# Idle TensorE products of the identity in three stretches of a two-layer gated attention and expert kernel

## What is computed

```python
x = x + tanh(g_xattn[0]) * attention0(layernorm(x), ctx)       # 16 heads attend to each other within a token
x = x + tanh(g_ffn[0])   * ffn0(layernorm(x))                  # 1024 wide, activations rounded to fp8
x = x + tanh(g_xattn[1]) * attention1(ctx, layernorm(x), mask) # 16 heads of 16, softmax over 512 keys
x = x + tanh(g_ffn[1])   * moe(layernorm(x))                   # 8 experts, top 2, 256 -> 1024 -> 256

# attention1: q, k, v = layernorm(. @ W + b) * scale + bias ; softmax(where(mask, q k / 4, -1e9)) v @ Wo + bo
# moe: logits = x @ gate_w + gate_b ; top 2 of the softmax, renormalised
#      out = sum over the two of weight * (silu(x @ w1) * (x @ w3)) @ w2
```

## Time and profile before

| what | value |
|---|---|
| median of 3 runs | 2118.34 us (2112.92 to 2119.60) |
| profiled execution | 2116.76 us |
| its span | 2115.0 us |
| mean granted TensorE clock | 0.954 of full |
| PE busy | 1902.5 us, 90% |
| DVE busy | 1563.4 us, 74% |
| ACT / POOL busy | 1156.6 us, 55% / 921.6 us, 44% |

### The profile page before, as it was taken

How to read it: one execution, slowest core, us unless ns; L and a number is a source line. 1 busy time by engine, 2 the same in 40 slices (tenths; PEclk the granted TensorE clock), 3 DMA queues, 4 the chain that set the end, 5 groups by cost and what they waited for, 6 DMA issues and landing times. The chain is left out here.

```text
span 2115.0 us, 36023 instructions
## 1 busy us (share of the span) xinstructions
PE 1902.5 (90%) x11968; PEld 1329.2 (63%) x11968; DVE 1563.4 (74%) x3233; ACT 1156.6 (55%) x2414; POOL 921.6 (44%) x683
## 2 busy tenths in 40 slices
PE   5899999986669999998999999929999999999998
PEld 2566666665223434343434343419999999999998
DVE  7999999993466677776767778547777777777775
ACT  2356665655335555655555655515555666666663
POOL 6999999981633334352434331112222222222222
PEclk8899999998679999999999999959999999999999
DMA  5222222210425151524242441037666666666661
GB/s 172 111 91 111 88 111 111 84 58 1 112 57 123 31 125 60 112 66 105 78 100 91 89 118 34 31 104 254 223 223 217 217 226 228 226 230 226 220 213 60
DMA packets 140067, 271.47 MB, mean 128 GB/s; under 512 B 13915, under 2 KB 91823, under 8 KB 134066
## 3 DMA queue, kind: packets, MB, share of 16 engines
q1 hardware_dynamic: 128812, 244.55, 37.6%
q0 software_dynamic: 10624, 25.26, 3.2%
q10 hardware_dynamic: 518, 0.27, 0.0%
HBM read 201.96 MB, written 71.39 MB: 129 GB/s over the span
## 5 line engine op out<-in xcount | busy, mean ns | idle before, releaser
L1447 DVE CUSTOM_DVE_ANT_0 x_dump<-x_ps,x_bias_q 128x512 bf16<-128x512 f32 x512 | 353.0, 689 | 103.5 <-PE x_ps L1140 90.4
L1316 ACT ACTIVATE x_PT<-x_ps 128x512 f32<-128x512 f32 x512 | 292.2, 601 | 231.5 <-PE x_ps L1155 228.7
L1929 ACT ACTIVATE X<-m_ps 128x256 f32<-128x256 f32 x312 | 119.1, 382 | 226.0 <-PE m_ps L1866 226.0
L1833 POOL DMA_INDIRECT out_dram<-e_y,e_label x78 | 78.9, 1011 | 362.5 <-DVE e_y L1985 350.6
L1140 PE MATMUL x_ps<-x_KS,x_QS 96*128 96x512 bf16 x512 | 200.7, 393 | 26.2 <-DVE x_mx L1447 25.7
L1154 PE MATMUL x_ps<-x_bias_k,x_ident_b 128*128 128x512 bf16 x512 | 196.8, 384 | 2.2 <-issue 1.1
L1155 PE MATMUL x_ps<-x_QS,x_KS 98*128 98x512 bf16 x512 | 196.5, 384 | 0.0
L1968 DVE TENSOR_TENSOR X<-X,m_ps 128x256 f32<-128x256 f32 x312 | 120.5, 416 | 97.0 <-ACT X L1929 92.5
L1866 PE MATMUL m_ps<-e_x_lo,m_hi 128*128 128x256 f32 x640 | 181.3, 283 | 1.5 <-DVE e_x_lo L1953 1.5
L1866 PE MATMUL m_ps<-e_x_hi,m_hi 128*128 128x256 f32 x640 | 180.9, 283 | 0.0
L1866 PE MATMUL m_ps<-e_x_hi,m_lo 128*128 128x256 f32 x640 | 180.7, 282 | 0.0
(11 more groups left out here) (309 smaller groups left out, 5462.9 us busy)
## 6 DMA issues: line engine op xcount, KB each, us to landing
m_raw<-in_L_ffn_w_dram SPq DMA_DIRECT2D x117, 1024.0 KB, 5.2
expert_in<-a_blank SPq DMA_DIRECT2D x34, 1032.0 KB, 4.3
parts<-x_part SPq DMA_DIRECT2D x24, 512.0 KB, 3.8
m_x<-expert_in SPq DMA_DIRECT2D x39, 258.0 KB, 4.8
next_mask_k<-in_maskT_dram SPq DMA_DIRECT2D x32, 256.0 KB, 2.6
next_mask_q<-in_mask_dram SPq DMA_DIRECT2D x29, 256.0 KB, 2.8
x_KS<-parts SPq DMA_DIRECT2D x16, 384.0 KB, 11.0
x_QS<-parts SPq DMA_DIRECT2D x8, 576.0 KB, 6.4
```

Of the source, the lines that this page charges most:

```text
L1316: act.activation(PT[unit % 2][:, k, :], ps_st[e % 3], ACT.Exp, scale=DH ** -0.5).then_inc(exp_done, 1)
L1447: dve.tensor_tensor_reduce(out=dump[:, :], in0=ps_max[m % 2], in1=bias_q[b % 2][:, q, :], scale=1.0, scalar=NEG, op0=ALU.add, op1=ALU.max, ...
L1929: act.activation(silu[f % 2], ps_h[f % 4][:, 0:BLK], ACT.Silu).then_inc(silu_done, 1)
```

## The change

A helper `stay_busy` on PE issues float32 products of the identity with itself, 128x128, into a bank that is not in use. The products wait for nothing of their own, they only stand in PE's order:

- In the units before 0: 6 ahead of `turn_x` of tiles 0 to 3 (unit -14), 38 ahead of tile 4's (-10), 9 ahead of tile 4's `turn_qk` (-8), 8 ahead of tile 5's `turn_x` (-6), 6 ahead of tile 5's `turn_qk` (-4), 6 ahead of tile 6's `turn_x` (-2), 4 each ahead of `project_kv(4)` and `project_kv(5)`, and one behind each of the maxima 0 to 23: 105 products. They write `ps_o`, and so PE also waits for the first of DVE's constants.
- In the last batch: 2 ahead of each of the four outputs, 10 and 2 ahead of the two turns, 3 ahead of each of the two logits, 10 ahead of the ranks: 36 products.
- In the block ahead of the experts: 16 products once ACT has made the high part of the second weight matrix.

```diff
--- before.py
+++ after.py
@@ -692,6 +692,7 @@
 Q_RUNS = ((0, 3, 0), (3, 2, 0), (5, 1, 0))
 K_RUNS = ((0, 2, 0), (2, 2, 0), (4, 1, 0), (5, 1, 2))
 READS = len(Q_RUNS) + len(K_RUNS)
+BUSY_BEFORE = {-14: 6, -10: 38, -8: 9, -6: 8, -4: 6, -2: 6}
 FIRST_UNIT, LAST_UNIT = -16, NUNITS + 15
 
 
@@ -888,6 +889,10 @@
                     if e[0] in ("spread", "output", "logits", "ranks"):
                         m_freed[e] = len(m_freed) + 2
 
+        final = TPB * (BATCH - 1)
+        BUSY_AT_LAST = {**{("output", final + j): 2 for j in range(TPB)}, ("turn", final // 2): 10, ("logits", final // 2): 3,
+                        ("turn", final // 2 + 1): 2, ("logits", final // 2 + 1): 3, ("ranks", BATCH - 1): 10}
+
         def wait(eng, semaphore, count):
 
             if count > 0:
@@ -1098,6 +1103,11 @@
 
         @block.tensor
         def _(pe):
+            def stay_busy(products, out):
+
+                for _ in range(products):
+                    pe.matmul(out, ident_f[:, :], ident_f[:, :], start=True, stop=True)
+
             def project_kv(n):
                 wait(pe, c_in[n % 2], 16 * (n // 2))
                 if n >= EARLY:
@@ -1170,6 +1180,8 @@
 
             def bank_m(event):
                 what, n = event
+                if event in BUSY_AT_LAST:
+                    stay_busy(BUSY_AT_LAST[event], ps_max[0][:, 0:P])
                 if what == "rows":
                     pe.wait_ge(max_split, n + 1)
                 elif what == "sums":
@@ -1226,6 +1238,7 @@
             pe.wait_ge(ahead.loaded, AHEAD)
             pe.wait_ge(ahead.bias3_in, 3 * 16)
             pe.wait_ge(consts, 1)
+            pe.wait_ge(consts_v, 1)
             for unit in UNITS_RUN:
                 maxima = iter(maxima_at(unit))
                 early, late = bank_m_events(unit)
@@ -1233,18 +1246,24 @@
                     if 0 <= unit < NUNITS:
                         scores(unit, k)
                     if k == (1 if unit >= 0 else 3):
+                        if unit < 0:
+                            stay_busy(BUSY_BEFORE.get(unit, 0), ps_o[:, 0:P])
                         for n in tiles_at(unit - 2):
                             turn_x(n)
                         for n in tiles_at(unit - 4):
                             turn_qk(n)
                     for m in islice(maxima, 1):
                         scores_for_maximum(m)
+                        if unit < 0:
+                            stay_busy(1, ps_o[:, 0:P])
                 for e in early:
                     bank_m(e)
                 if 0 <= unit - 1 < NUNITS:
                     values(unit - 1)
                 for n in tiles_at(unit - 2):
                     project_q(n)
+                if unit in (-12, -8):
+                    stay_busy(4, ps_o[:, 0:P])
                 for n in tiles_at(unit):
                     project_kv(n)
                 for e in late:
@@ -1730,6 +1749,12 @@
                         scatter_rows(pool, routing, xs, k, j)
                 pool.wait_ge(routing.scattered, 16 * NT * TOPK)
 
+            @block.tensor
+            def _(pe):
+                pe.wait_ge(hi_done[1], 1)
+                for _ in range(16):
+                    pe.matmul(ps[:, 7, 0:P], ident_f[:, :], ident_f[:, :], start=True, stop=True)
+
             @block.scalar
             def _(act):
                 for n in range(3):
```

## The result

The changed kernel takes 2102.24 us (median, 2101.20 to 2102.93) against 2118.84 us for the kernel before in the same comparison: a ratio of 0.9926, interval 0.9909 to 0.9942, that is 16.6 us (0.8%) faster by the medians and 0.7% by the ratio. The forecast was 2106.4 us, the range 2099 to 2114. The profiled execution has a span of 2099.3 us where before had 2115.0, and a mean granted clock of 0.975 where before had 0.954.

A forecast was written before the change was run, and what follows sets the result against it. Bound: PE's expert products, after three serial starts (units before 0, last batch's routing, way into the experts) slowed by half clock. 2116.76 - 4.9 - 3.6 - 1.9 = 2106.4 us; range 2099 to 2114.

The forecast's parts named there:

- The price of a product: One idle product on PE was taken to cost 0.23 us at full clock and 0.43 us at half.
- The first wait: PE's first product in the units before 0 waits for DVE's zeroing of the bank: +0.5 us.
- A1: First layer's last product to turn_x(4): query projections at full clock, counted at one half, -2.0 us; wait +0.5.
- A2: From turn_x(4) to the o_bias products behind project_kv(5): tile 4's chain now at full clock, -3.2 us.
- A3: From the o_bias products to unit 0's first values: tiles 5 and 6, gains against products outlasting waits, -0.2 us.
- B: Last values to the ranks in the last batch: outputs, turns and logits gain clock, -3.6 us.
- C: From the block ahead of the experts on: products +0.2, turn gains 0.5, expert product records 1.6, together -1.9 us.
- Rival 1: Every hole is held at full clock, in all three stages: -14.9 us, 2101.9 us; chance 0.17.
- Rival 2: The clock still falls in the gaps left: -5.0 us, 2111.8 us; chance 0.27 together with rivals 3 and 5.
- Rival 3: Transposes hold no clock, first projections and logits pairs not gained: -6.4 us, 2110.4 us; chance 0.27 with rivals 2 and 5.
- rival 4: Products outlast their waits at half clock, mainly the 38 ahead of turn_x(4): +19.4 us, 2136 us; chance 0.04.
- Rival 5: The start is hidden anyway by spread DMAs or POOL's masks: 2111.8 us; chance 0.27 with rivals 2 and 3.

The follow-up runs named there:

- a_only: Kernel before plus only the 105 products of the units before 0 and their wait: ratio 0.9966 (0.9952 to 0.9980).
- b_only: Kernel before plus only the 36 products in the last batch's outputs and routing: ratio 0.9982 (0.9968 to 0.9996).
- c_only: Kernel before plus only the 16 products ahead of the experts: ratio 0.9976 (0.9964 to 0.9989).
- all: The whole changed kernel run once more against the kernel before: ratio 0.9932 (0.9916 to 0.9948).
- no38: Changed kernel without the 38 products ahead of the turn of tile 4: 2109.38 us, ratio 0.9968 to the kernel before.
- turns: Changed kernel with two identity transposes for each idle product, except the 16 ahead of the experts: 2100.53 us, ratio 0.9926 to the kernel before.
- moved: Changed kernel with 14 products behind maximum 1 instead of one, 2 ahead of turn_x(5) instead of 8: 2102.40 us, ratio 0.9940 to the kernel before.
- after: Profiled execution of the changed kernel in the first comparison with the kernel before: span 2099.3 us against 2115.0.
- no_late: Changed kernel without what it adds in units -6 to -1 (8, 6, 6 and 24 single products): 2109.22 us, ratio 0.9959 to the kernel before.
- c_again: Kernel before plus only the 16 products ahead of the experts, timed a second time: ratio 0.9994 (0.9980 to 1.0008).
- mid: Changed kernel with products moved into its remaining holes, plus 6 zero-weight products ahead of seven batches' first logits: 2095.36 us, ratio 0.9898 to the kernel before.

## Why the prediction was right, and where its sizes were off

- **The bound** was right: three serial starts whose gains arrive whole. Apart from leg M, a_only moves its own legs alone, b_only and c_only likewise.
- **The price of a product**, 0.23 and 0.43 us: measured 0.230 and 0.42. The prediction's remark that weight loads of the same length at either clock would make the sum 2.0 us lower does not follow: its own count by columns alone gives 0.42 us at half clock, so shorter loads would leave the price of the nine products as it is.
- **The first wait**, +0.5: PE's first key product waits 0.6 us longer (4.92 for 4.30), inside leg A1.
- **A1**, "I count it at one half: -2.0", with +0.5 for the wait: the leg is two-valued. With the clock held through the first query projections it is -3.9 (all, no38, turns, moved), without -0.9 (after, a_only, no_late). The forecast was -3.5 for the one value and +0.5 for the other, so the first price was near and the second 1.4 us too high, as the clock rises in the second projection rather than after the fourth. Four of the seven profiles held it, close to the one half, and the mean is -2.6 where -1.5 was forecast. The sign "DVE's scale and shift beginning 2 to 4 us earlier" is met in all (3.9 us, counted from the first layer's last product) and missed in after (0.9).
- **A2**, -3.2: measured -3.2 in every profile with the 38 products. Their own share is only 1.7, since the nine behind them raise the clock by themselves (no38).
- **A3**, -0.2: measured -1.0. The nine products ahead of `turn_x(5)` cost 2.1 and not 2.7 us. Taking all late products out loses 1.3 us in this leg, so they pay for themselves in spite of that cost.
- **B**, -3.6: measured -4.1 to -4.4 in six profiles and -4.7 in the seventh (moved). As forecast the first output is at half clock and its follower waits for products; the third and fourth are at full. The second, counted at one half, still took 1.91 us. From the first output to the first turn the profile of after is 1.7 us shorter than before's where 2.1 were forecast. From the first turn to the ranks it is 2.6 shorter where 1.5 were forecast: the second pair of turn and logits, counted at one half, was held in every profile, and the two products ahead of the second turn, charged in full, cost nothing that shows. The two errors have opposite signs.
- **C**, -1.9: right for after (-2.1), mis-sized in general. Over the eight profiles with the 16 products the leg is -0.6 on the average (-2.1 to +1.1), and two steps failed. The first is "with a rise in between about 5.5: +0.2". In six of the eight the next block began 0.9 to 1.5 us later behind DVE's last low part than in before, because the clock rose late and the 32 records outlasted the block. In four of them it was more than 1 us, which the prediction itself had named as a sign of being wrong. The second is "then the turn gains 0.5 and the product records 1.6", which took for granted that the clock survives the hole of 1.5 us behind the turn. It did in five profiles; in three (all, no38, no_late) the first expert products ran at half clock.
- **The sum**, -10.4, was 4 to 6 us short of the medians. By the mean legs of the profiles with each part, A gives -2.6 - 3.2 - 1.0, B -4.4, C -0.6: -11.8. Against the forecast that is 1.1 more in A1, 0.8 in A3, 0.8 in B and 1.3 less in C, so part of the agreement is errors that cancel. -11.8 is inside the interval of all (-11.0 to -17.8 us) but near its upper edge. Leg M is 1.1 to 2.5 us shorter than before's in six of the seven profiles that have stage A's products in full or but for one group, and 3.8 longer in the seventh; without those products it goes from -3.1 to +4.6. Whether the change has a share in it, through the moment at which unit 0 begins, these single profiles don't settle. What is shown is that the scatter is of the size of the gap: c_only and c_again, one kernel, differ by 4.3 us.
- **The rivals.** Rival 1 gave 2101.9 us, nearest to the measured time, but not for its reason: the profile of after held neither the first projections nor the first two outputs. Its argument that a hole of 1.5 us alone is not followed by a fall was misread: before's own trace has one behind a wait of 1.58 us (at 758 us, above). Rival 2 is refuted by the last batch, where both pairs of turn and logits were held in every profile, though three profiles show, as it said, the first expert products still at half clock. Rival 3 is refuted by turns, rival 4 by the clock's rise within the products (no38: nine in 3.19 us). Rival 5 is refuted by legs A1 to A3 arriving at the first values.

## What to carry to other kernels

Where a serial chain runs through a TensorE that waits, fill its waits with idle products that are ready at once and end before the wait does. Put them into the hole that lets the clock fall, not behind it: nine behind a hole of 3.8 us ran at half clock and cost 2.1 us, fourteen inside it ran at full. Compare the time between two fixed instructions rather than the whole time, and in several profiles, since falls of the clock elsewhere differ from execution to execution by as much as the effect of one part; a part whose median moved by 5 us moved by 1.3 when timed again.

## What was not expected of the hardware

- 76 float32 transposes of the identity in 8.51 us kept the granted clock at 1.00 just as 76 product records in 8.75 us did.
- With six products of all-zero weights in a wait of 1.58 us of each of seven batches, the one profile (mid) has no half clock in 711 us, where the same code without them had 3.4 to 20.4 us; the mean clock of all executions moved only from 0.980 to 0.982. That such products hold the clock is likely by this, not shown.
- The same kernel's leg A1 has two lengths 3.0 us apart, by whether the clock falls at about 545 us, with the same instructions ahead of it.
